# Attention: three sums of sixteen moved from VectorE to TensorE, a ring of twelve places, the product with v eight units behind

## The chip, the cores and the metric

The kernel runs on one core of one Trainium2 chip. The metric is device time in microseconds (us) of the whole kernel. The engines that matter here are TensorE (PE in the profile; PEld is its loading of weights), VectorE (DVE), ScalarE (ACT), GpSimd (POOL) and SyncE (SP), which issues most DMAs. Each engine takes its instructions strictly in the order in which they are written and waits for the others by semaphores.

## The reference, cut to what matters

The reference is four residual layers on x of shape (8, 256, 16, 16). The change lies in the second, an attention with 32 heads of 8 channels and 256 positions. The softmax runs over the batch (`axis=0`), not over the keys:

```python
qkv = jnp.einsum('brnd,ed->brne', xr, w_qkv) + b_qkv
q, k, v = jnp.split(qkv, 3, axis=-1)
attn = jnp.einsum('brnd,brmd->brnm', q, k)
attn = jax.nn.softmax(attn, axis=0)
out = jnp.einsum('brnm,brmd->brnd', attn, v)
```

So for each head and each pair of positions eight numbers are exponentiated and divided by their sum: maximum and sum go over the eight batches, element by element.

## The kernel before, in words

**Units.** A unit is one head and one 128 x 128 block of its positions (keys on the partitions, queries along the row), for all eight batches: 128 x 1024 numbers. A head has four units, four heads make a group of 16 units (`UPG`), and eight groups (`NG`) make 128 units (`UNITS`). U is the unit's number, u its place in its group.

**What is done to a unit.** TensorE computes the scores with eight bf16 matmuls into two of the eight PSUM banks (`scores`, L1684; three units have room, `SLOT`). VectorE takes the maximum over the batches (`maximum`, L1042). TensorE subtracts it with two matmuls by a negated identity (`subtract`, L1693). ScalarE takes the exponential into a place of the ring `e_ring` in SBUF (`exponentials`, L644). VectorE sums over the batches (`total`, L1049). ScalarE takes the logarithm of the sum and the exponential of its negative, which is the reciprocal (`logarithm` L649, `inverse` L655). GpSimd multiplies the unit by it in place (`weights`, L459). TensorE multiplies it with v into bank 6, eight fp32 matmuls, four of them side by side on 32 columns each (`product`, L1712).

**Order.** `attention_steps` runs every engine through turns. In turn U TensorE issues the scores of U, the subtraction of U-1 and the product of U-5 (`LAG`); VectorE the maximum of U and the sum of U-1; ScalarE the exponential of U-1, then logarithm and inverse of U-2; GpSimd the weights in the order of U. Nothing is reordered. The ring has eight places (`ER`): the exponential of U waits until the product of U-8 has read its place. The reciprocals have four places (`RS`).

**Once in a group.** After the product of a group's last unit ScalarE copies bank 6 to SBUF (`evacuate`, L664), TensorE transposes it in four matmuls into bank 7 (`transpose_heads`, L1723), and VectorE adds that to x (`add_heads`, L1068, seven times; the eighth group follows the last unit in halves). In the kernel before that is in turns 4, 6 and 7 of the next group.

**Beginning and end.** The q and k parts lie first in the ring and in `scratch`, and SyncE stores them to DRAM, from `scratch` in two DMAs of 1536 KB; a wait of SyncE (L388) stands for both before it loads the second group's heads (L361). At the end VectorE multiplies half of unit 126 and all of unit 127 itself (`normalise_last`, L1054).

## Time and profile before

| what | us |
|---|---|
| median of 3 runs (lowest, highest) | 599.51 (599.00, 599.76) |
| profiled execution, its own time | 600.21 |
| its span in the profile | 598.2 |
| busy in the span: TensorE, VectorE | 504.8 (84%), 481.1 (80%) |
| busy in the span: ScalarE, GpSimd | 328.3 (55%), 387.7 (65%) |
| attention, first maximum to last product | 91.3 to 392.1 |

The span is what the profiler recorded of one execution; 2.0 us of that execution's own time lie outside it. The shares are means over layers with different limits: in the attention stretch VectorE and GpSimd are busy nearly all the time, after it TensorE is. Starts of the matmuls are recorded and their ends are modelled, so a step of TensorE is best read from one start to the next.

### The profile page before, as it was taken

The page shows a single profiled execution, that of the slowest core. Times are in us where ns is not written, and L with a number is a line of the kernel's source. Part 1 is how long each engine was busy: PE and PEld are TensorE (multiplying, and loading weights), DVE is VectorE, ACT ScalarE, POOL GpSimd, SP SyncE. Part 2 cuts the span into 40 slices and gives each one's busy share as a digit, 9 for nine tenths or more (in the row PEclk, how much of TensorE's full clock was granted, in tenths as well). Part 3 has the DMA queues.
Part 4 walks back from the last instruction along what each step waited for, and adds up shares of the span by engine and source line. Part 5 has one row for each costly group of instructions (what it writes and reads, how often), then busy time and mean ns, then how long its engine had stood idle before and what let it go on. Part 6 is the DMA issues. An engine that isn't in the chain of part 4 may idle for free.

```text
span 598.2 us, 13058 instructions
## 1 busy us (share of the span) xinstructions
PE 504.8 (84%) x4610; PEld 308.1 (52%) x4611; DVE 481.1 (80%) x876; ACT 328.3 (55%) x709; POOL 387.7 (65%) x243
## 2 busy tenths in 40 slices
PE   3999687877877778777777877799999999999996
PEld 1554354444444444444444444468986656656665
DVE  5658967999999999999999999978777873333455
ACT  3624674676676766767667676624433533333341
POOL 3200483999899998999999899923105267766640
PEclk9998895999899999999999899999999999999999
DMA  7130257244243332332433320000013223322276
GB/s 225 37 110 1 85 167 253 81 124 130 78 112 84 94 105 73 112 98 80 106 88 93 96 78 2 2 1 1 2 55 101 71 75 107 99 87 90 83 290 211
DMA packets 34288, 56.62 MB, mean 95 GB/s; under 512 B 8541, under 2 KB 21494, under 8 KB 34102
## 3 DMA queue, kind: packets, MB, share of 16 engines
q1 hardware_dynamic: 28950, 43.95, 24.8%
q0 software_dynamic: 3744, 10.39, 5.6%
q10 hardware_dynamic: 1536, 1.51, 0.8%
q8 instruction: 37, 0.61, 0.4%
q14 instruction: 21, 0.17, 0.1%
HBM read 38.43 MB, written 17.40 MB: 93 GB/s over the span
## 4 chain that ended last, share of the span: by engine, by line
PE 37%; POOL 29%; DVE 17%; issue 10%; ACT 3%; DMA 3%; POOLq 0%; SPq 0%; ACTq 0%; DVEq 0%
POOL e_ring L459 29%; PE ps L1890 12%; PE ps L1911 6%; DVE m_bf L1042 4%; DVE x_hat L1049 4%; PE ps L1693 2%; PE ps L1820 2%; DVE stats L865 2%; PE ps L1879 2%; ACT e_ring L644 1%; PE ps L1900 1%; PE ps L1590 1%; PE ps L1621 1%; PE ps L1839 1%; PE ps L1767 1%
## 5 line engine op out<-in xcount | busy, mean ns | idle before, releaser
L459 POOL TENSOR_TENSOR e_ring<-e_ring,x_hat 128x1024 f32<-128x1024 f32 (+1 forms) x127 | 269.8, 2127 | 30.7 <-ACT x_hat L655 18.5
L644 ACT ACTIVATE e_ring<-ps 128x1024 f32<-128x1024 f32 x128 | 131.1, 1025 | 89.7 <-PE ps L1693 89.5
L1042 DVE TENSOR_REDUCE m_bf<-ps 128x128 bf16<-128x1024 f32 x128 | 154.9, 1211 | 4.2 <-PE ps L1684 4.2
L1049 DVE TENSOR_REDUCE x_hat<-e_ring 128x128 f32<-128x1024 f32 x128 | 154.5, 1207 | 3.2 <-ACT e_ring L644 3.2
L1693 PE MATMUL ps<-m_bf,ident_neg 128*128 128x512 bf16 x256 | 82.2, 404 | 61.7 <-DVE m_bf L1042 61.5
L1712 PE MATMUL ps<-e_ring,v_slot 128*32 128x128 f32 x2048 | 86.5, 286 | 1.1 <-POOL e_ring L459 0.6
L1684 PE MATMUL ps<-q_stack,k_stack 72*128 72x128 bf16 x1024 | 83.4, 227 | 3.9 <-DMA k_stack<-qk_parts 3.9
L1712 PEld LDWEIGHTS ps<-e_ring,v_slot 128*32 128x32 f32 x2048 | 50.4, 110 | 58.0 <-issue 51.1
L1684 PEld LDWEIGHTS ps<-q_stack,k_stack 72*128 72x128 bf16 x1024 | 61.9, 101 | 32.0 <-issue 25.8
L1890 PE MATMUL ps<-w_sb,e_ring 128*128 x156 | 74.0, 598 | 1.3 <-ACT e_ring L744 0.8
L477 POOL DMA_INDIRECT e_ring<-token_rows,slot_x x39 | 37.7, 966 | 43.2 <-DVE slot_y L1331 29.5
L1693 PEld LDWEIGHTS ps<-m_bf,ident_neg 128*128 128x128 bf16 x256 | 15.6, 100 | 82.2 <-DVE m_bf L1042 82.0
L1407 DVE TENSOR_TENSOR scratch<-ps,e_ring 128x256 f32<-128x256 f32 x39 | 16.5, 424 | 47.9 <-ACT e_ring L750 47.6
L483 POOL DMA_INDIRECT pair_rows<-scratch,slot_y x37 | 37.8, 1020 | 25.7 <-DVE scratch L1414 14.7
L750 ACT ACTIVATE e_ring<-ps 128x256 f32<-128x256 f32 x39 | 15.0, 384 | 50.0 <-PE ps L1890 49.8
L655 ACT ACTIVATE x_hat<-x_hat 128x128 f32<-128x128 f32 x128 | 39.6, 309 | 4.0
L1911 PE MATMUL ps<-w_sb,scratch 128*128 x156 | 40.5, 382 | 1.2 <-issue 0.6
L649 ACT ACTIVATE x_hat<-x_hat 128x128 f32<-128x128 f32 x128 | 38.5, 301 | 0.7 <-DVE x_hat L1049 0.7
L1890 PEld LDWEIGHTS ps<-w_sb,e_ring 128*128 128x128 f32 x156 | 26.6, 190 | 22.1 <-issue 21.9
L453 POOL TENSOR_TENSOR e_ring<-e_ring 128x512 bf16<-128x512 f32 x8 | 9.1, 1158 | 42.0 <-ACT e_ring L588 41.7
L744 ACT ACTIVATE e_ring<-ps 128x256 f32<-128x256 f32 x39 | 14.9, 383 | 27.8 <-PE ps L1879 27.8
L1911 PEld LDWEIGHTS ps<-w_sb,scratch 128*128 128x128 f32 x156 | 26.7, 190 | 4.7 <-issue 2.7
(237 smaller groups left out, 674.2 us busy)
## 6 DMA issues: line engine op xcount, KB each, us to landing
q_stack<-qk_parts SPq DMA_DIRECT2D x32, 288.0 KB
k_stack<-qk_parts SPq DMA_DIRECT2D x32, 288.0 KB
w_sb<-in_w13T_dram SPq DMA_DIRECT2D x16, 256.0 KB, 7.6
qk_parts<-e_ring SPq DMA_DIRECT2D x8, 384.0 KB, 3.4
qk_parts<-scratch SPq DMA_DIRECT2D x2, 1536.0 KB, 19.7
x_res<-in_x_dram SPq DMA_DIRECT2D x8, 256.0 KB, 3.9
w_sb<-in_w2T_dram SPq DMA_DIRECT2D x8, 256.0 KB, 7.5
work<-pair_rows SPq DMA_DIRECT2D x8, 256.0 KB, 4.7
```

Of the source, the lines that this page charges most:

```text
L459: nc.gpsimd.tensor_tensor(ev, ev, view(x_hat, CH + (u % RS) * P, [[0, quads], [1, P], [0, 2]]), ALU.mult).then_inc(norm_done, 1)
L483: nc.gpsimd.indirect_dma_start(out=y_dram[:, :], in_=y_rows[:, k % YR], in_offset=None, out_offset=bass.IndirectOffsetOnAxis(ap=slot_y[:, ...
L644: nc.scalar.activation(e_ring[:, u % ER, :].rearrange("p (q n k) -> p q n k", q=BQ, k=2), view(ps, 2 * (v % SLOT) * CH, [[2 * P, BQ], [1, ...
L649: nc.scalar.activation(s_ln[:, u % 2], s_sum[:, u % 2], ACT.Ln).then_inc(ln_done, 1)
L655: nc.scalar.activation(s_inv[:, u % RS], s_ln[:, u % 2], ACT.Exp, scale=-1.0).then_inc(r_done, 1)
L1042: nc.vector.tensor_reduce(m_bf[:, u % 2], view(ps, 2 * (v % SLOT) * CH, [[1, P], [P, B]]), AX, ALU.max).then_inc(max_done, 1)
L1049: nc.vector.tensor_reduce(s_sum[:, u % 2], by_position(e_ring[:, u % ER, :]), AXY, ALU.add).then_inc(sum_done, 1)
L1684: last = nc.tensor.matmul(view(ps, 2 * (v % SLOT) * CH + b * P, [[1, P]]), k_stack[:, i, b * N + mh * P:b * N + (mh + 1) * P], q_stack[:, ...
L1693: last = nc.tensor.matmul(bank(2 * (v % SLOT) + j), ident_neg[:], view(m_bf, (u % 2) * P, [[0, B // 2], [1, P]]), start=False, stop=True, ...
L1712: last = nc.tensor.matmul(ps[32 * (b % 4):32 * (b % 4) + 32, 6, (b // 4) * N + nh * P:(b // 4) * N + (nh + 1) * P], v_slot[:, b * H + mh, ...
L1890: last = nc.tensor.matmul(bank(r % 2), x_turned[:, r % 2, h * P:(h + 1) * P], w13_sb[:, h, bass.ds(e * (2 * C), 2 * C)], start=(h == 0), s ...
L1911: last = nc.tensor.matmul(ps[:, 6 + r % 2, 0:C], gated_t[:, r % 2, f * P:(f + 1) * P], w2_sb[:, f, bass.ds(e * C, C)], start=(f == 0), sto ...
```

## The change: what it does

Three things are changed together. **Sums on TensorE:** for the units with u = 0, 5 and 10 (in the first group 5 and 10, in the last only 0; 21 units in all) the sum over the batches is no longer VectorE's. TensorE adds the eight batch blocks into bank 7 with eight fp32 matmuls by the identity (`partial_sum`), four in turn U+2 and four in turn U+3, each four behind the subtraction and ahead of the product of that turn; ScalarE takes the logarithm straight from PSUM at the beginning of turn U+4. Bank 7 is also where the heads are transposed, so the sum of u = 10 waits for `add_heads`, and the transposes for the logarithm of u = 5. **Lags:** VectorE's other 107 sums come two turns behind their unit (one turn for units 0 to 4), logarithm and inverse a turn later, and the product eight turns behind. Evacuation, transposes and `add_heads` move to turns 7, 10 and 11. **Room:** the ring gets twelve places, the last four in `scratch`; the exponential of unit 8, the first that is put there, waits for the two stores out of `scratch`. The reciprocals get eight places. At the end VectorE multiplies unit 125 as well; GpSimd's loop is written out.

```diff
-    ER = 8
-    LAG = 5
-    RS = 4
+    RING, MORE = 8, 4
+    ER = RING + MORE
+    LAG = 8
+    RS = 8
+    TURN_AT = 10
...
+        def attention_steps(step):
+            for U in range(UNITS + LAG):
+                step(U, lambda k: 0 <= U - k < UNITS)
+        def summed_on_pe(U):
+            return U % UPG in ((5, 10) if U < UPG else (0,) if U // UPG == NG - 1 else (0, 5, 10))
+        DVE_SUMS = [U for U in range(UNITS) if not summed_on_pe(U)]
+        PE_SUMS = [U for U in range(UNITS) if summed_on_pe(U)]
+        SUM_BANK, SUM_STEPS, SUM_AT = 7, 2, 2
+        DVE_LAST = {UNITS - 3: 0, UNITS - 2: BQ // 2, UNITS - 1: 0}
+        def sum_step(U):
+            return U + (1 if U < PE_SUMS[0] else 2)
+        def slot_of(U):
+            k = U % ER
+            return (e_ring, k * UW) if k < RING else (scratch, (k - RING + 1) * UW)
...
+                nc.gpsimd.tensor_tensor(ev, ev, view(x_hat, CH + (p % RS) * P, [[0, quads], [1, P], [0, 2]]), ALU.mult
                                         ).then_inc(norm_done, 1)
-            with pool.Fori(0, NG - 1) as g:
-                for u in range(UPG):
-                    weights(g * UPG + u, u)
-            for u in range(UPG - 2):
-                weights((NG - 1) * UPG + u, u)
-            weights(UNITS - 2, UPG - 2, BQ // 2)
+            for p in range(UNITS):
+                if p not in DVE_LAST:
+                    weights(p)
+                elif DVE_LAST[p]:
+                    weights(p, DVE_LAST[p])
...
+                if U >= ER:
                     act.wait_ge(pv_done, U - ER + 1)
-                elif U == 2:
+                elif U in (2, RING):
+                    h = 0 if U == 2 else 1
                     for s in range(2):
-                        act.wait_ge(parts_out[s], 16 * NCH)
-                nc.scalar.activation(e_ring[:, u % ER, :].rearrange("p (q n k) -> p q n k", q=BQ, k=2),
-                                     view(ps, 2 * (v % SLOT) * CH, [[2 * P, BQ], [1, P], [P, 2]]), ACT.Exp).then_inc(exp_done, 1)
-            def logarithm(U, u):
-                act.wait_ge(sum_done, U + 1)
-                nc.scalar.activation(s_ln[:, u % 2], s_sum[:, u % 2], ACT.Ln).then_inc(ln_done, 1)
-            def inverse(U, u):
+                        act.wait_ge(parts_out[2 * h + s], 16 if h else 16 * NCH)
...
+            def logarithm(U):
+                if summed_on_pe(U):
+                    act.wait_ge(pe_sum_done, PE_SUMS.index(U) + 1)
+                    total = ps[:, SUM_BANK, 0:P]
+                else:
+                    act.wait_ge(sum_done, DVE_SUMS.index(U) + 1)
+                    total = s_sum[:, DVE_SUMS.index(U) % 2]
+                nc.scalar.activation(s_ln[:, U % 2], total, ACT.Ln).then_inc(ln_done, 1)
...
+            def attention_step(U, has):
+                g, u = U // UPG, U % UPG
+                late = U - SUM_AT - SUM_STEPS
+                if 0 <= late < UNITS and summed_on_pe(late):
+                    logarithm(late)
+                    inverse(late)
                 if has(1):
-                    exponentials(U - 1, v - 1, (u - 1) % UPG)
-                if has(2):
-                    logarithm(U - 2, (u - 2) % UPG)
-                    inverse(U - 2, (u - 2) % UPG)
-                if u == LAG - 1 and has(LAG):
+                    exponentials(U - 1)
+                for done in (U - 2, U - 3):
+                    if 0 <= done < UNITS and not summed_on_pe(done) and sum_step(done) + 1 == U:
+                        logarithm(done)
+                        inverse(done)
+                if u == LAG - 1 and g >= 1:
                     evacuate(g)
-                if u in (0, 1, 2, LAG) and has(u + 1) and has(0):
...
+                n = DVE_SUMS.index(U)
+                if n >= 2:
+                    dve.wait_ge(ln_done, DVE_SUMS[n - 2] + 1)
+                nc.vector.tensor_reduce(s_sum[:, n % 2], ring(U, [[2, P], [2 * P, BQ], [1, 2]]), AXY, ALU.add).then_inc(sum_done, 1)
...
+                    maximum(U)
+                for done in (U - 1, U - 2):
+                    if 0 <= done < UNITS and not summed_on_pe(done) and sum_step(done) == U:
+                        total(done)
+                if u == TURN_AT + 1 and 1 <= g < NG:
                     add_heads(g, g)
-            attention_steps(dve, attention_step)
-            normalise_last(UNITS - 2, BQ // 2)
-            normalise_last(UNITS - 1, 0)
+            attention_steps(attention_step)
+            for U, first in DVE_LAST.items():
+                normalise_last(U, first)
...
+            def partial_sum(U, step):
+                n = PE_SUMS.index(U)
+                if step == 0:
+                    pe.wait_ge(exp_done, U + 1)
+                    if n >= 1:
+                        pe.wait_ge(ln_done, PE_SUMS[n - 1] + 1)
+                    if U % UPG == 10 and U >= UPG:
+                        pe.wait_ge(x2_added, U // UPG)
+                for b in range(step * (B // SUM_STEPS), (step + 1) * (B // SUM_STEPS)):
+                    last = nc.tensor.matmul(ps[:, SUM_BANK, 0:P], ident[:],
+                                            ring(U, [[2, P]], (b // 2) * (2 * P) + b % 2),
+                                            start=(b == 0), stop=(b == B - 1))
+                if step == SUM_STEPS - 1:
+                    last.then_inc(pe_sum_done, 1)
+            def product(U):
...
+                if summed_on_pe(group * UPG + 5):
+                    pe.wait_ge(ln_done, (group * UPG + 5) + 1)
...
                 if has(0):
-                    scores(U, v, u, g)
+                    scores(U)
                 if has(1):
-                    subtract(U - 1, v - 1, (u - 1) % UPG)
+                    subtract(U - 1)
+                for step in range(SUM_STEPS):
+                    summed = U - SUM_AT - step
+                    if 0 <= summed < UNITS and summed_on_pe(summed):
+                        partial_sum(summed, step)
                 if has(LAG):
-                    product(U - LAG, (u - LAG) % UPG, g)
-                if isinstance(U, int) and U == UNITS + 2:
+                    product(U - LAG)
+                if U == UNITS + LAG - 3:
                     keep_busy(IDLE_BANK, 1)
-                if u == LAG + 1 and has(LAG + 2):
+                if u == TURN_AT and 1 <= g < NG:
                     transpose_heads(g)
```

The instructions of TensorE around the addition of the heads in the second group, first of the kernel before (L1684 scores, L1693 subtraction, L1712 product; turn 24):

```order
L1684 MATMUL ps<-q_stack,k_stack 128x128 [waits exp_done,stack_in2]
L1684 MATMUL ps<-q_stack,k_stack 128x128 x7
L1693 MATMUL ps<-m_bf,ident_neg 128x512 [waits max_done]
L1693 MATMUL ps<-m_bf,ident_neg 128x512
L1712 MATMUL ps<-e_ring,v_slot 32x128 [waits norm_done]
L1712 MATMUL ps<-e_ring,v_slot 32x128 x7
```

and of the change (L1714 scores, L1723 subtraction, L1738 the new sum by the identity, L1758 product; from the subtraction of turn 28 on):

```order
L1723 MATMUL ps<-m_bf,ident_neg 128x512 [waits max_done]
L1723 MATMUL ps<-m_bf,ident_neg 128x512
L1738 MATMUL ps<-e_ring,ident 128x128 [waits x2_added,ln_done,exp_done]
L1738 MATMUL ps<-e_ring,ident 128x128 x3
L1758 MATMUL ps<-scratch,v_slot 32x128 [waits norm_done,v_slot_ready1]
L1758 MATMUL ps<-scratch,v_slot 32x128 x7
L1714 MATMUL ps<-q_stack,k_stack 128x128 [waits exp_done]
L1714 MATMUL ps<-q_stack,k_stack 128x128 x7
L1723 MATMUL ps<-m_bf,ident_neg 128x512 [waits max_done]
L1723 MATMUL ps<-m_bf,ident_neg 128x512
L1738 MATMUL ps<-e_ring,ident 128x128 x4
L1758 MATMUL ps<-scratch,v_slot 32x128 [waits norm_done]
```

Four matmuls of the sum now stand between the subtraction and the product, and the next scores stand behind them; the first four of this unit wait for `x2_added`, the end of `add_heads`.

VectorE at the same place, before (L1042 maximum, L1049 sum, L1068 `add_heads`; turns 23 and 24):

```order
L1042 TENSOR_REDUCE m_bf<-ps 128x128 [waits sub_done,scores_done]
L1049 TENSOR_REDUCE x_hat<-e_ring 128x128 [waits ln_done,exp_done]
L1068 TENSOR_TENSOR x_res<-x_res,ps 128x16x32 [waits acc_tr]
L1042 TENSOR_REDUCE m_bf<-ps 128x128 [waits sub_done,scores_done]
L1049 TENSOR_REDUCE x_hat<-e_ring 128x128 [waits ln_done,exp_done]
```

and in the change (L1068 is now the maximum, L1076 the sum, L1095 `add_heads`; turns 27 to 29):

```order
L1068 TENSOR_REDUCE m_bf<-ps 128x128 [waits sub_done,scores_done]
L1076 TENSOR_REDUCE x_hat<-e_ring 128x128 [waits ln_done,exp_done]
L1095 TENSOR_TENSOR x_res<-x_res,ps 128x16x32 [waits acc_tr]
L1068 TENSOR_REDUCE m_bf<-ps 128x128 [waits sub_done,scores_done] x2
L1076 TENSOR_REDUCE x_hat<-e_ring 128x128 [waits ln_done,exp_done]
```

Where a sum has gone to TensorE two maxima follow each other, here right behind `add_heads`.

## Rows read from the trace of the kernel before

**Rows 1.** Windows, one group: length; busy of PE, PEld, DVE, ACT, POOL; clock; DMA
```profile
244.80:281.50 36.70, 28.50 (x422) 15.63 (x423) 36.70 (x34) 25.78 (x54) 34.15 (x17) 1.00 0.36 95
```
**Rows 2.** Timeline of VectorE at an `add_heads`: start, duration, line, operation
```profile
258.11 0.67 DVE L1068 TENSOR_TENSOR x_res<-x_res,ps 128x512 f32<-128x512 f32 x1
258.71 1.21 DVE L1042 TENSOR_REDUCE m_bf<-ps 128x128 bf16<-128x1024 f32 x1
259.84 1.21 DVE L1049 TENSOR_REDUCE x_hat<-e_ring 128x128 f32<-128x1024 f32 x1
```
**Rows 3.** Timeline of TensorE, one turn behind that `add_heads`; idle time in brackets
```profile
259.98 0.61 PE L1693 MATMUL ps<-m_bf,ident_neg 128*128 128x512 bf16 x2 [1.10 <-DVE m_bf L1042]
260.51 0.66 PE L1712 MATMUL ps<-e_ring,v_slot 128*32 128x128 f32 x16
261.11 0.62 PE L1684 MATMUL ps<-q_stack,k_stack 72*128 72x128 bf16 x8
262.23 0.61 PE L1693 MATMUL ps<-m_bf,ident_neg 128*128 128x512 bf16 x2 [0.50 <-DVE m_bf L1042]
```
**Rows 4.** Timeline of TensorE at the lower clock, and the turn after it
```profile
151.25 1.04 PE L1693 MATMUL ps<-m_bf,ident_neg 128*128 128x512 bf16 x2 [0.50 <-DVE m_bf L1042]
152.22 1.08 PE L1712 MATMUL ps<-e_ring,v_slot 128*32 128x128 f32 x16
153.24 1.03 PE L1684 MATMUL ps<-q_stack,k_stack 72*128 72x128 bf16 x8
154.06 0.85 PE L1693 MATMUL ps<-m_bf,ident_neg 128*128 128x512 bf16 x2
...
155.45 0.62 PE L1684 MATMUL ps<-q_stack,k_stack 72*128 72x128 bf16 x8
155.91 0.60 PE L1693 MATMUL ps<-m_bf,ident_neg 128*128 128x512 bf16 x2
```
**Rows 5.** Windows of TensorE: length, busy, granted clock, DMA
```profile
152.00:154.00 2.00, 2.00 (x25) 0.50 0.13 51
223.00:224.00 1.00, 1.00 (x6) 0.50 0.45 117
336.00:337.00 1.00, 1.00 (x10) 0.50 0.20 70
```
**Rows 6.** The line of `add_heads`: ns min/median/max, first and last start
```profile
L1068 DVE TENSOR_TENSOR x_res<-x_res,ps x7: 671/674/676, 147.1 to 368.6; 128x512 f32<-128x512 f32 x7
```
**Rows 7.** Timeline of TensorE, fp32 matmuls of 128 columns (two records each)
```profile
76.73 0.61 PE L1630 MATMUL ps<-qkv_sb,x_hat 128*128 128x128 f32 x4
77.17 1.02 PE L1621 MATMUL ps<-x_hat,qkv_sb 128*128 128x512 f32 x2
...
84.09 0.68 PE L1630 MATMUL ps<-qkv_sb,x_hat 128*128 128x128 f32 x4 [0.24 <-DVE work L979]
84.61 1.02 PE L1621 MATMUL ps<-x_hat,k_wT_sb 128*128 128x512 f32 x2
```
**Rows 8.** The line of the maximum: ns min/median/max, first and last start
```profile
L1042 DVE TENSOR_REDUCE m_bf<-ps x128: 1205/1211/1225, 91.3 to 385.0; 128x128 bf16<-128x1024 f32 x128
```
**Rows 9.** SyncE's waits: total, times, longest; then its next issue
```profile
SPq L388 <- DMA qk_parts<-scratch: 20.7, 1, 20.7
...
116.80 0.72 SPq L361 DMA_DIRECT2D q_stack<-qk_parts  x1
```
**Rows 10.** Timeline of ScalarE: the exponential of unit 8
```profile
112.93 1.02 ACT L644 ACTIVATE e_ring<-ps 128x1024 f32<-128x1024 f32 x1 [0.69 <-PE ps L1693]
```
**Rows 11.** Timeline, the last weights on VectorE and the last product
```profile
389.10 2.29 DVE L1054 TENSOR_TENSOR e_ring<-e_ring,x_hat 128x512 f32<-128x512 f32 x2
...
391.44 0.66 PE L1712 MATMUL ps<-e_ring,v_slot 128*32 128x128 f32 x16 [0.47 <-DVE e_ring L1054]
```
**Rows 12.** Chain that ended last: GpSimd's weights without a wait between
```profile
158.68 2.01 POOL e_ring L459
160.78 2.15 POOL e_ring L459
```

More of the change, by code:

```diff
@@ L292, in slot_steps, with ring @@
                 step(s, s % XR, inside)
-        def attention_steps(eng, step):
-            for u in range(UPG):
-                step(u, u, u, 0, lambda k: k <= u)
-            for U in range(UPG, UNITS):
-                step(U, U, U % UPG, U // UPG, lambda k: True)
-            for u in range(LAG):
-                step(UNITS + u, UNITS + u, u, NG, lambda k: k > u)
+        def attention_steps(step):
[12 more added lines that the diff above has]
+            return (e_ring, k * UW) if k < RING else (scratch, (k - RING + 1) * UW)
+        def ring(U, dims, first=0):
+            buf, at = slot_of(U)
+            return view(buf, at + first, dims)
         def score_banks(v):
@@ L313, in row_bank @@
             return 5 if j < B // 2 else 4 + j % 2
-        def later_than(U, k):
-            return not isinstance(U, int) or U >= k
-        assert (SLOTS - 7) % XR == 0 and UPG % ER == 0
+        assert (SLOTS - 7) % XR == 0 and CH <= UW and (MORE + 1) * UW <= 6144
         block = ctx.enter_context(nc.Block())
@@ L1069, in add_heads, with attention_step @@
                                         ALU.add).then_inc(x2_added, 1)
-            def attention_step(U, v, u, g, has):
+            def attention_step(U, has):
+                g, u = U // UPG, U % UPG
                 if has(0):
-                    maximum(U, v, u)
-                if has(1):
-                    total(U - 1, (u - 1) % UPG)
-                if u == LAG + 2 and has(LAG + 3):
+                    maximum(U)
[3 more added lines that the diff above has]
+                if u == TURN_AT + 1 and 1 <= g < NG:
                     add_heads(g, g)
-            attention_steps(dve, attention_step)
-            normalise_last(UNITS - 2, BQ // 2)
-            normalise_last(UNITS - 1, 0)
+            attention_steps(attention_step)
+            for U, first in DVE_LAST.items():
+                normalise_last(U, first)
             dve.wait_ge(x2_added, NG - 1)
@@ L1675, in _, with scores @@
                 qk_tile(n)
-            def scores(U, v, u, g):
+            def scores(U):
+                g, u = U // UPG, U % UPG
                 i, mh, nh = u // 4, (u // 2) % 2, u % 2
@@ L1688, in scores, with subtract @@
                 last.then_inc(scores_done, 1)
-            def subtract(U, v, u):
+            def subtract(U):
                 pe.wait_ge(max_done, U + 1)
                 for j in range(2):
-                    last = nc.tensor.matmul(bank(2 * (v % SLOT) + j), ident_neg[:],
-                                            view(m_bf, (u % 2) * P, [[0, B // 2], [1, P]]), start=False, stop=True,
+                    last = nc.tensor.matmul(bank(2 * (U % SLOT) + j), ident_neg[:],
+                                            view(m_bf, (U % 2) * P, [[0, B // 2], [1, P]]), start=False, stop=True,
@@ new lines, in product @@
+            def product(U):
+                grp, u = U // UPG, U % UPG
+                i, mh, nh = u // 4, (u // 2) % 2, u % 2
+                if U % 4 == 0:
+                    pe.wait_ge(v_slot_ready[i], grp + 1)
+                if U % UPG == 0 and U >= 1:
+                    pe.wait_ge(acc_out, grp)
+                if U in DVE_LAST:
+                    pe.wait_ge(norm_last, list(DVE_LAST).index(U) + 1)
+                    if DVE_LAST[U]:
+                        pe.wait_ge(norm_done, UNITS - len(DVE_LAST) + 1)
@@ L1713, in product @@
                                             v_slot[:, b * H + mh, i, :],
-                                            view(e_ring, (u % ER) * UW + (b // 2) * (2 * P) + b % 2, [[2, P]]),
-                                            start=(u == 0 and b < 4), stop=(u == UPG - 1), skip_group_check=True)
+                                            ring(U, [[2, P]], (b // 2) * (2 * P) + b % 2),
+                                            start=(U % UPG == 0 and b < 4), stop=(U % UPG == UPG - 1), skip_group_check=True)
                 last.then_inc(pv_done, 1)
```

60 lines of the change are left out of this document (24 added, 36 removed).

## Prediction

> **What bounds the kernel now.** I read the windows first: in a group of 16 turns VectorE is busy in all of the 36.70 us, GpSimd in 34.15, TensorE in 28.50, ScalarE in 25.78 [rows 1]. The timeline of VectorE then shows no gap: instructions follow each other by 1.13, behind `add_heads` by 0.60 [rows 2]; 32 x 1.128 + 0.60 = 36.7, the whole group. So VectorE sets the pace, a turn is 2.26, and the other engines wait for it: TensorE idles 0.50 before each subtraction, 1.10 behind `add_heads` [rows 3]. GpSimd takes a turn when it need not wait in 2.10 [rows 12], 33.6 a group.
>
> **What the sums cost where they leave.** 21 sums of 1.128 go, 23.7 us. VectorE keeps 128 maxima and 107 sums, 235 x 1.128 = 265.1, and seven `add_heads` of 0.60 [rows 2, 6], 4.2: 269.3 in all. That is the gain if nothing else waits. A group with three fewer is 33.3, about GpSimd's 33.6, so all three engines come close together and what counts is who waits for whom.
>
> **What a sum costs on TensorE.** Eight fp32 matmuls of 128 columns, four to a turn; I call four a piece. The trace has two such matmuls between neighbours in 0.44 [rows 7], so 0.88 for a piece, and in 0.52 behind a wait, so 1.04. What the hand-over from a subtraction adds no row shows; I take 0.93, which is nearest to the undisturbed row, and keep 0.88 and 1.04 as the ends.
>
> **What waits for a piece.** From rows 3 and 4: maximum's start to subtraction 1.27, subtraction to product 0.53, product to scores 0.60, scores to subtraction 0.46 when nothing is awaited (155.45 to 155.91), scores' start to the next maximum 0.65 (0.62 and a signal). A turn of TensorE is thus 1.59, with a piece 2.52, against VectorE's 2.26, or 1.13 in the turn without a sum. Queued behind the piece are the product and the next scores, and VectorE's next maximum waits for these.
>
> Let s be a unit summed on TensorE and 0 the subtraction of s+1, in turn s+2. The maximum of s+1 began at -1.27, that of s+2 at 0.99; without a sum between, VectorE is ready for that of s+3 at 2.12. TensorE: piece 0.53 to 1.46, product to 2.06, scores of s+3, ready at 2.71. VectorE waits 0.59. Next turn: subtraction 2.52, piece 3.05 to 3.98, product to 4.58, scores ready at 5.23; VectorE (2.71 + 2.26) is ready at 4.97 and waits 0.26. In the turn after that scores are ready at 6.82, VectorE at 7.49: over. So a sum saves 1.13 and costs 0.85.
>
> For u = 10 in groups 1 to 6 the first piece also waits for `add_heads`, which stands between the sum of u = 9 and the maximum of u = 12: it begins at 0.99, ends 0.67 later, and the piece starts at 1.70 instead of 0.53. Product, scores and subtraction stand behind it. The maximum of 13 can start at 3.88 while VectorE is ready at 2.72: 1.16, and 0.26 in the next turn. 1.42 for 1.13 saved.
>
> Of the 21 units, 6 are of this second kind, 15 of the first; I count unit 5 with the start. 14 x 0.85 + 6 x 1.42 = 20.4.
>
> **Start.** The exponential of unit 8 now waits for the stores out of `scratch`; SyncE's wait for these ends at 116.80, while the exponential ran at 112.93 before [rows 9, 10]. With 1.02 it ends at 117.9. Behind it on ScalarE are logarithm and inverse of unit 6 and later exponentials; three units of scores fit into PSUM, so TensorE stops before scores 11. VectorE can by then have done maxima 0 to 10 and seven sums, 18 x 1.128 = 20.3, since 91.3 [rows 8]: 26.6 passed, 6.3 idle. GpSimd gets unit 6 only at about 118.5; 119 weights at 2.10 from there end at 368, earlier than VectorE needs them.
>
> **End.** VectorE's last sum ends at 91.3 + 269.3 + 6.3 + 20.4 = 387.3; before it began the weights at 389.10 [rows 11]. It now does one more whole unit, 1.2 (an estimate: the pair took 2.29, half of it possibly waiting), so the last product starts at 387.3 + 1.2 + 2.29 + 0.05 = 390.8 against 391.44 [rows 11], 0.6 earlier. The transposes in turn 10, the copy in turn 7 and the twelve places cost and bring nothing: the idle 0.50 [rows 3] covers four transposes of 0.11 (an estimate by one record of rows 7), and GpSimd never kept TensorE waiting in a steady turn. If that cover goes, about 0.4 a group is added.
>
> The Trainium skill bears on the unit added at the end: by SBUF — State Buffer, section "SBUF: two separate sides", a VectorE operation with two SBUF inputs and a GpSimd operation exclude each other for a whole instruction. The trace fits in that half a unit and a whole one took 2.29 [rows 11], about as much as two whole ones. By that rule the sum would be later by up to one instruction of GpSimd, 2.1 [rows 12].
>
> **The clock.** At the lower clock a turn takes 0.97 + 1.02 + 0.82 = 2.81 instead of 1.59 [rows 4]. Its falls were short (granted clock 0.50 [rows 5]) and came shortly after three of the seven `add_heads`: these run from 147.1 to 368.6 [rows 6], so some 36.9 apart, the third near 220.9 and the sixth near 331.7. Behind each of the seven TensorE idles as in rows 3. Before, TensorE's spare hid nearly all of it. Now the idling before the piece of u = 10 is as long (subtraction's end 0.60 to 1.70) and the fall would meet pieces. If it begins with the first piece, that takes 1.86, product 1.02, scores are ready at 5.64; the second piece at full clock 0.93, the maximum of 14 at 8.11 instead of 6.40: 1.7. If it begins with the subtraction of 12 it is 1.6. Six places x 3/7 x 1.65 = 4.2.
>
> The Trainium skill (TensorE: Matmul & The Clock Gate, section "Why this matters for your kernels") warns only of longer idle gaps; by it no fall is due here and the time would be that of the second rival below. The trace disagrees, three times.
>
> **Sum.** The profiled execution took 600.21, the median is 0.7 lower. 600.2 - 0.6 + 4.2 = 603.8; against the median 603.1.
>
> **Rivals.** *Pieces are hidden.* If the scores come in time after all, the 20.4 go: 599.5 - 0.6 - 20.4 = 578.5, where GpSimd's 33.6 a group is nearly the bound too. For it: TensorE would be busy only 28.5 + 6 x 0.93 = 34.1 of 36.7. Against it: the order of TensorE's queue. Chance 0.13; half hidden, about 589, 0.17.
> *The clock stays up* because the pieces fill TensorE: 599.5 - 0.6 = 598.9, with pieces of 0.88 2.0 less (20 sums x 2 x 0.05). 0.17. This is also the change without effect.
> *Every one of the six gaps brings a fall*, with pieces of 1.04: 598.9 + 6 x 1.65 + 20 x 2 x 0.11 = 613. The longer idle stretch and the start, where TensorE waits some 2 us for the exponential of 8, speak for it; 0.08. It decides as soon as four gaps bring falls, 605.5.
> My forecast, some falls: 0.45, own range 600 to 608.
>
> **Numbers.** About 0.2% (1.2 us) is what can be told from no change. Faster: 0.30 and a little of the third case, 0.33. Same: 0.14. Slower: 0.53. The range reaches from 586, which leaves out most of the first rival, to 610.
>
> **What would show it.** Right: VectorE idle before the maxima of s+3 (0.6, and 1.2 behind `add_heads`) with scores as releaser, a group at about 36 us, the piece at 0.93, the exponential of unit 8 at 116.8, falls of the granted clock at turn 12 with a group of some 38. Wrong: a group under 35 us with VectorE or GpSimd gapless, or the clock at 1.00 throughout.

## Result and profile after

The changed kernel took 607.06 us (median of 4 runs, 606.53 to 609.06) against 599.25 for the one before beside it (4 runs, 598.88 to 599.76): a ratio of 1.0136, 95% interval 1.0111 to 1.0161. It is slower by 7.8 us; forecast were 3.6. The profiled execution of after took 606.7 for a span of 604.9; that of before 600.21 for 598.2. In the profiles, which the rest compares, the difference of the spans is 6.7. One execution of g1 below took 854.93 at a granted clock of 0.56, where its others had 0.96 or more; it is left out of every number.

Four points of the trace split the span: VectorE's first maximum, its last, and the first addition of the last heads behind the last product (L1061 before, L1088 after).

| stretch | before | after | change | forecast |
|---|---|---|---|---|
| start of the program to the first maximum | 91.35 | 89.92 | -1.43 | 0 |
| first to last maximum | 293.64 | 297.07 | +3.43 | +2.0 |
| last maximum to the addition of the last heads | 8.09 | 11.91 | +3.82 | +1.6 |
| from there to the end | 205.12 | 206.00 | +0.88 | 0 |
| span | 598.2 | 604.9 | +6.70 | +3.6 |

The forecast column is worked out from the prediction's own sums: VectorE ready at 387.3 + 4.2, less four instructions of 1.128, puts the last maximum at 386.99; last product at 390.8 + 4.2, and 1.64 from there to the addition, as before.

Windows of after, one group with the granted clock at full speed and one with a fall (columns as in [rows 1], which they answer):

```profile
203.28:239.93 36.65, 32.59 (x476) 21.92 (x468) 33.90 (x31) 25.70 (x54) 33.80 (x17) 1.00 0.34 95
239.93:278.09 38.16, 34.09 (x476) 22.96 (x468) 33.90 (x31) 25.68 (x54) 33.78 (x17) 0.96 0.34 91
```

VectorE has three instructions fewer and 2.8 us less work, but the group is as long as before: 2.75 us of it are now gaps. No engine is busy throughout, so the bound is a chain between two. The waits (total, times, longest) name it:

```profile
PE ps L1723 <- DVE m_bf L1068: 27.7, 53, 1.8
DVE m_bf L1068 <- PE ps L1714: 25.6, 25, 2.9
```

TensorE waits for the maximum, and the maximum for TensorE's scores; before, only the first of the two was of weight (the second came to 4.2). VectorE behind `add_heads` (L1095), answering to [rows 2]:

```profile
229.76 0.68 DVE L1095 TENSOR_TENSOR x_res<-x_res,ps 128x512 f32<-128x512 f32 x1
230.35 1.22 DVE L1068 TENSOR_REDUCE m_bf<-ps 128x128 bf16<-128x1024 f32 x1
232.92 1.22 DVE L1068 TENSOR_REDUCE m_bf<-ps 128x128 bf16<-128x1024 f32 x1 [1.34 <-PE ps L1714]
234.06 1.21 DVE L1076 TENSOR_REDUCE x_hat<-scratch 128x128 f32<-128x1024 f32 x1
235.40 1.23 DVE L1068 TENSOR_REDUCE m_bf<-ps 128x128 bf16<-128x1024 f32 x1
```

and TensorE beside it, answering to [rows 3]; L1738 is a piece (four fp32 matmuls, two records each):

```profile
228.78 0.61 PE L1723 MATMUL ps<-m_bf,ident_neg 128*128 128x512 bf16 x2 [0.50 <-DVE m_bf L1068]
230.59 1.15 PE L1738 MATMUL ps<-scratch,ident 128*128 128x128 f32 x8 [1.21 <-DVE x_res L1095]
231.66 0.66 PE L1758 MATMUL ps<-e_ring,v_slot 128*32 128x128 f32 x16
232.26 0.62 PE L1714 MATMUL ps<-q_stack,k_stack 72*128 72x128 bf16 x8
232.72 0.60 PE L1723 MATMUL ps<-m_bf,ident_neg 128*128 128x512 bf16 x2
233.15 1.07 PE L1738 MATMUL ps<-scratch,ident 128*128 128x128 f32 x8
234.15 0.66 PE L1758 MATMUL ps<-e_ring,v_slot 128*32 128x128 f32 x16
```

The maxima of 230.35 and 232.92 have no sum between them, so VectorE would be back after 1.13; it comes back after 2.57 and waits 1.34 by the row, which counts the maximum as 1.22. The reason is the order of one queue: the scores at 232.26 need nothing of the piece or of the product ahead of them, but stand behind both, and the piece stood 1.21 until `add_heads` had read the bank.

In three of the six groups with this place the granted clock fell there, to 0.50 (the level of 1.2 GHz), while pieces ran. TensorE in one of them, answering to [rows 4], and windows of the other two, answering to [rows 5] (length, busy of five engines, clock, DMA):

```profile
192.44 1.82 PE L1738 MATMUL ps<-e_ring,ident 128*128 128x128 f32 x8 [1.20 <-ACT e_ring L661]
194.20 1.08 PE L1758 MATMUL ps<-e_ring,v_slot 128*32 128x128 f32 x16
195.21 1.03 PE L1714 MATMUL ps<-q_stack,k_stack 72*128 72x128 bf16 x8
```
```profile
268.00:272.00 4.00, 4.00 (x37) 3.04 (x37) 1.42 (x3) 0.49 (x1) 2.13 (x2) 0.60 0.36 102
305.00:309.00 4.00, 3.61 (x32) 2.99 (x33) 1.38 (x2) 0.76 (x3) 3.28 (x2) 0.57 0.58 166
305.39:308.20 2.81, 2.81 (x24) 2.34 (x24) 0.99 (x1) 0.37 (x2) 2.81 (x2) 0.50 0.64 176
```

The first row names ScalarE as the releaser; but the exponential that ended at 192.30 is the next unit's, which the piece does not need, and `add_heads` ended at 192.30 too. In all six groups the piece began 0.14 or 0.15 behind the end of `add_heads`.

Piece 1.76, product 1.01, scores 1.03: the interval between the two maxima was 4.07 in this fall, against 2.56 or 2.57 in the three groups without one. From maximum to maximum the eight groups took 37.72, 37.11, 36.71, 37.17, 36.71, 36.71, 37.06, 34.45 before (the last has 15 intervals) and 38.58, 36.64, 38.14, 36.65, 38.16, 38.12, 36.64, 34.14 after.

The end of attention, answering to [rows 11]: VectorE, GpSimd, TensorE.

```profile
386.99 1.22 DVE L1068 TENSOR_REDUCE m_bf<-ps 128x128 bf16<-128x1024 f32 x1
388.12 3.47 DVE L1076 TENSOR_REDUCE x_hat<-e_ring 128x128 f32<-128x1024 f32 x3
391.50 3.75 DVE L1081 TENSOR_TENSOR e_ring<-e_ring,x_hat 128x1024 f32<-128x1024 f32 x3
...
389.16 3.29 POOL L477 TENSOR_TENSOR e_ring<-e_ring,x_hat 128x1024 f32<-128x1024 f32 x2 [0.61 <-ACT x_hat L677]
...
393.58 0.69 PE L1758 MATMUL ps<-e_ring,v_slot 128*32 128x128 f32 x16 [1.44 <-DVE e_ring L1081]
394.20 2.08 PE L1666 MATMUL ps<-ones_sb 128*128 128x512 f32 x2
396.20 1.70 PE L1758 MATMUL ps<-e_ring,v_slot 128*32 128x128 f32 x32
```

VectorE is through with the weights at 395.25. The products of units 126 and 127 do not follow: a filler matmul (L1666, there to keep TensorE busy) is in the queue ahead of them, and takes 2.08 at the lower clock instead of 1.13. The same filler in the kernel before, and the clock from VectorE's last weights to the addition of the heads in the changed one (0.69; before, 1.00):

```profile
389.08 1.13 PE L1637 MATMUL ps<-ones_sb 128*128 128x512 f32 x2
```
```profile
395.26:398.90 3.64, 3.64 (x40) 2.00 (x39) 1.53 (x7) 0.66 (x2) 0.00 (x0) 0.69 0.00 0
```

### The profile page after: what moved, and what is told of

Same layout as the page of the kernel before. It is cut to its first block, busy times and chain, and to the rows that moved or that the text cites. A ratio compares the mean times of both kernels' runs of the same rounds, so it can differ in the third digit from the quotient of the medians.

```text
span 604.9 us, 13580 instructions
## 1 busy us (share of the span) xinstructions
PE 537.5 (89%) x4946; PEld 357.2 (59%) x4947; DVE 463.0 (77%) x856; ACT 327.7 (54%) x709; POOL 383.2 (63%) x242
## 4 chain that ended last, share of the span: by engine, by line
PE 61%; DVE 22%; DMA 8%; issue 5%; ACT 2%; SPq 1%; POOL 0%; DVEq 0%; ACTq 0%
PE ps L1943 11%; DVE m_bf L1068 9%; PE ps L1758 7%; PE ps L1723 7%; PE ps L1738 7%; PE ps L1714 6%; PE ps L1964 6%; DVE x_hat L1076 4%; DMA qk_parts<-scratch 3%; PE ps L1619 2%; PE ps L1873 2%; PE ps L1932 2%; PE ps L1953 1%; DMA k_stack<-qk_parts 1%; PE ps L1892 1%
## 5 line engine op out<-in xcount | busy, mean ns | idle before, releaser
L477 POOL TENSOR_TENSOR e_ring<-e_ring,x_hat 128x1024 f32<-128x1024 f32 x86 | 181.0, 2128 | 32.6 <-ACT x_hat L677 32.3
L1068 DVE TENSOR_REDUCE m_bf<-ps 128x128 bf16<-128x1024 f32 x128 | 155.9, 1219 | 28.2 <-PE ps L1714 25.6
L661 ACT ACTIVATE e_ring<-ps 128x1024 f32<-128x1024 f32 x88 | 90.1, 1024 | 64.7 <-PE ps L1723 64.3
L1723 PE MATMUL ps<-m_bf,ident_neg 128*128 128x512 bf16 x256 | 80.3, 396 | 27.8 <-DVE m_bf L1068 27.7
L1076 DVE TENSOR_REDUCE x_hat<-e_ring 128x128 f32<-128x1024 f32 x74 | 89.4, 1210 | 1.3 <-ACT e_ring L661 1.3
L477 POOL TENSOR_TENSOR scratch<-scratch,x_hat 128x1024 f32<-128x1024 f32 x40 | 84.7, 2141 | 5.4 <-ACT x_hat L677 5.3
L1714 PE MATMUL ps<-q_stack,k_stack 72*128 72x128 bf16 x1024 | 82.7, 226 | 4.0 <-DMA k_stack<-qk_parts 3.1
L1714 PEld LDWEIGHTS ps<-q_stack,k_stack 72*128 72x128 bf16 x1024 | 61.5, 101 | 31.9 <-issue 25.1
L1758 PE MATMUL ps<-e_ring,v_slot 128*32 128x128 f32 x1408 | 59.0, 287 | 2.1 <-DVE e_ring L1081 1.4
L661 ACT ACTIVATE scratch<-ps 128x1024 f32<-128x1024 f32 x40 | 40.9, 1023 | 28.2 <-PE ps L1723 25.2
L1758 PEld LDWEIGHTS ps<-e_ring,v_slot 128*32 128x32 f32 x1408 | 35.1, 110 | 30.8 <-issue 16.2
L677 ACT ACTIVATE x_hat<-x_hat 128x128 f32<-128x128 f32 x128 | 39.8, 311 | 4.1
L1723 PEld LDWEIGHTS ps<-m_bf,ident_neg 128*128 128x128 bf16 x256 | 17.9, 100 | 38.2 <-DVE m_bf L1068 37.6
L1076 DVE TENSOR_REDUCE x_hat<-scratch 128x128 f32<-128x1024 f32 x33 | 40.0, 1211 | 0.2 <-ACT x_hat L671 0.2
L1738 PEld LDWEIGHTS ps<-e_ring,ident 128*128 128x128 f32 x224 | 32.4, 206 | 10.8 <-ACT e_ring L661 6.7
```

The lines of the kernel that those rows point to most:

```text
L477: nc.gpsimd.tensor_tensor(ev, ev, view(x_hat, CH + (p % RS) * P, [[0, quads], [1, P], [0, 2]]), ALU.mult).then_inc(norm_done, 1)
L661: nc.scalar.activation(ring(U, [[2 * P, BQ], [2, P], [1, 2]]), view(ps, 2 * (U % SLOT) * CH, [[2 * P, BQ], [1, P], [P, 2]]), ACT.Exp).then ...
L677: nc.scalar.activation(s_inv[:, U % RS], s_ln[:, U % 2], ACT.Exp, scale=-1.0).then_inc(r_done, 1)
L1068: nc.vector.tensor_reduce(m_bf[:, U % 2], view(ps, 2 * (U % SLOT) * CH, [[1, P], [P, B]]), AX, ALU.max).then_inc(max_done, 1)
L1076: nc.vector.tensor_reduce(s_sum[:, n % 2], ring(U, [[2, P], [2 * P, BQ], [1, 2]]), AXY, ALU.add).then_inc(sum_done, 1)
L1714: last = nc.tensor.matmul(view(ps, 2 * (U % SLOT) * CH + b * P, [[1, P]]), k_stack[:, i, b * N + mh * P:b * N + (mh + 1) * P], q_stack[:, ...
```

## Experiments

Each is the changed kernel with the edit shown; times are medians, ratios against the kernel before on the same chip (medians 598.7 to 599.3). "End" is the stretch from the last maximum to the addition of the last heads.

**e1. No sums on TensorE.** Lags, ring and end stay.

```diff
-            return U % UPG in ((5, 10) if U < UPG else (0,) ...
+            return False
-            return U + (1 if U < PE_SUMS[0] else 2)
+            return U + (1 if U < 5 else 2)
```

> Keeps the lags, the twelve places, the wait of unit 8 and the end of the change, but gives all 128 sums back to VectorE. Theory (the pieces stand ahead of the next scores in TensorE's queue, and the piece behind add_heads meets falls of the clock): VectorE is gapless again, a group takes 36.7 us, no fall costs more than 0.5; what stays against the kernel before is start and end, so 599 to 604 us. Rival (the lags, the places in scratch and the later product cost the time, not the sums): still 605 or more.

604.97, ratio 1.0099 (1.0070 to 1.0128). The groups 1 to 6 are what the theory said:

```profile
203.80:240.52 36.72, 29.51 (x424) 16.19 (x420) 36.72 (x35) 25.63 (x54) 33.31 (x17) 0.95 0.32 90
```

VectorE gapless at 36.7, and a clock of 0.95 in this group that costs nothing, since TensorE has spare. But the time is all but the rival's 605. The first group took 39.68 (37.72 before), and from the last maximum to the addition of the heads 11.83 (8.09 before): 5.7 us in the two, without a single sum on TensorE. My theory had the sums right and these two places wrong. In the first group it is the exponential of unit 8, the stretch of [rows 9, 10]:

```profile
116.24 1.02 ACT L661 ACTIVATE scratch<-ps 128x1024 f32<-128x1024 f32 x1 [4.78 <-DMA qk_parts<-scratch]
```

**e2. Third sum away from `add_heads`.** u = 13 instead of 10.

```diff
-            return U % UPG in ((5, 10) if U < UPG else (0,) if U // UPG == NG - 1 else (0, 5, 10))
+            return U % UPG in ((5, 13) if U < UPG else (0,) if U // UPG == NG - 1 else (0, 5, 13))
```

> The change with the third sum of each group at u = 13 instead of 10, so that its first piece in turn 15 no longer waits for add_heads in turn 11; the number of matmuls is the same. Theory: each third sum costs VectorE 0.8 us of waiting instead of 1.65 (6 x 0.85 = 5), and the 1.2 us of idling before the piece and with it the three falls of 1.5 us go: 596 to 600 us, the group at 35.8. Rival (TensorE is simply too full, with 24 more fp32 matmuls a group): no change, 605 to 608.

597.66, ratio 0.9963 (0.9940 to 0.9986), as expected. Groups 2 to 6 took 35.87 to 35.89, with the clock at 1.00:

```profile
201.64:237.51 35.87, 32.36 (x469) 22.00 (x468) 33.88 (x30) 25.55 (x53) 33.86 (x17) 1.00 0.36 98
```

Against the 36.64 without a fall this is 0.77, the second kind of wait turned into the first; against 38.1 it is 2.3. From the first to the last maximum 288.97 instead of 297.07: 8.1 us, six of 0.77 and three falls of 1.5 make 9.1, and one fall is left in group 1 (36.72 instead of 35.88).

The end changed too, though nothing there was edited: 10.28 instead of 11.91. The filler still stands ahead of the last two products, but the clock stayed at 1.00:

```profile
386.17 0.67 PE L1758 MATMUL ps<-e_ring,v_slot 128*32 128x128 f32 x16 [2.23 <-DVE e_ring L1081]
386.76 1.13 PE L1666 MATMUL ps<-ones_sb 128*128 128x512 f32 x2
387.82 1.13 PE L1758 MATMUL ps<-e_ring,v_slot 128*32 128x128 f32 x32
```
```profile
387.85:389.92 2.07, 2.07 (x39) 1.51 (x39) 1.53 (x6) 0.66 (x2) 0.00 (x0) 1.00 0.00 0
```

VectorE's last weight ended at 387.85, so the filler was over by then, and from there to the addition it took 2.07, where the changed kernel took 3.64 (1.69 before the change). In f2 and f3 below the clock stayed at 1.00 there as well, and the same stretch took 2.08 in each.

**e3. Scores ahead of the piece.** The scores of the next unit are issued right behind the subtraction.

```diff
-                if has(0):
-                    scores(U)
+                if U == 0:
+                    scores(0)
                 if has(1):
                     subtract(U - 1)
+                if has(-1):
+                    scores(U + 1)
```

> The change with one thing moved: TensorE issues the scores of U+1 right behind the subtraction of U-1, ahead of the pieces and of the product; same instructions, same number. Theory: the next maximum no longer waits for a piece, the 21 us of VectorE's waits go, a group comes down to what GpSimd needs, 33.6 to 34.5 us, and the time to 582 to 590. Rival (TensorE's total work, or contention, is the bound): the waits only move to another place and the time stays above 600.

582.62, ratio 0.9705 (0.9667 to 0.9743). All of the change's sums stay, only the order in TensorE's queue is another, and the gaps on VectorE are gone:

```profile
196.84:230.17 33.33, 31.85 (x470) 22.64 (x469) 33.33 (x32) 25.76 (x53) 33.33 (x17) 1.00 0.39 104
```

33.33 is the 33.3 that the prediction gave for 32 - 3 instructions and an `add_heads`. VectorE and TensorE around a unit summed on TensorE:

```profile
209.25 1.23 DVE L1068 TENSOR_REDUCE m_bf<-ps 128x128 bf16<-128x1024 f32 x1
210.38 1.22 DVE L1076 TENSOR_REDUCE x_hat<-e_ring 128x128 f32<-128x1024 f32 x1
211.51 2.36 DVE L1068 TENSOR_REDUCE m_bf<-ps 128x128 bf16<-128x1024 f32 x2
...
210.54 0.61 PE L1723 MATMUL ps<-m_bf,ident_neg 128*128 128x512 bf16 x2 [0.26 <-DVE m_bf L1068]
210.98 0.61 PE L1714 MATMUL ps<-q_stack,k_stack 72*128 72x128 bf16 x8
211.43 1.12 PE L1738 MATMUL ps<-e_ring,ident 128*128 128x128 f32 x8
```

Two maxima in one stretch of 2.36: the scores at 210.98 are in time, and the piece takes what TensorE had to spare. VectorE and GpSimd are now both busy throughout. This is the forecast's first rival (pieces hidden), which lacked only the order.

**e4. Old end.** The unit added to VectorE's last weights goes back to GpSimd.

```diff
-        DVE_LAST = {UNITS - 3: 0, UNITS - 2: BQ // 2, UNITS - 1: 0}
+        DVE_LAST = {UNITS - 2: BQ // 2, UNITS - 1: 0}
```

> The change with the end of the kernel before: GpSimd multiplies unit 125 again and VectorE only half of 126 and 127. Theory (VectorE's weights of unit 125 wait for GpSimd's running instruction and take 2.0 us, and the filler matmul behind runs at the lower clock): last product 2 to 3 us sooner after the last maximum, 603.5 to 605.5 us. Rival (the end is as long either way, because GpSimd is later with 125 than VectorE): 606 to 608.

608.89, ratio 1.0147 (1.0103 to 1.0192): no gain, the theory on the end falls. The unit was not what made the end longer (11.79 from the last maximum to the addition, against 11.91): VectorE is 0.8 later with its last weight, and TensorE takes 0.9 less behind it. The line of VectorE's last weights (ns min/median/max), after and here:

```profile
L1081 DVE TENSOR_TENSOR e_ring<-e_ring,x_hat x3: 679/1212/2019, 391.5 to 394.0; 128x1024 f32<-128x1024 f32 x2, 128x512 f32<-128x512 f32 x1
```
```profile
L1081 DVE TENSOR_TENSOR e_ring<-e_ring,x_hat x2: 2177/2311/2445, 393.3 to 395.7; 128x512 f32<-128x512 f32 x1, 128x1024 f32<-128x1024 f32 x1
```

Beside GpSimd's weights half a unit and a whole one take over 2.1; with GpSimd done, 0.68 and 1.21. This run had four falls in its six groups.

**f1. Scores ahead, ring of eight, product seven behind.** The edit of e3, and:

```diff
-    RING, MORE = 8, 4
+    RING, MORE = 8, 0
-    LAG = 8
+    LAG = 7
```

> The scores-ahead version (582.6 us) with the ring cut back to eight places and the product with v seven units behind. Exponential 8 then writes a place of the first eight and waits for no store. Theory (the lags and the room cost time at the start only because exponential 8 waits for the scratch stores): the first group, 41.1 us in the scores-ahead run with one interval of 4.49, falls to about 37 to 39, the later groups stay at 33.3, and the time is 578 to 581. Rival (eight places are too few once VectorE turns a unit every 1.1 us without a sum, so that exponentials wait for products): groups of 34 us or more, and a time of 583 or more.

580.41, ratio 0.9701 (0.9661 to 0.9741). The first group went from 38.89 to 36.52, the later ones stayed at 33.34: eight places are enough, and the wait for the stores was avoidable. The end was 1.5 longer (13.59 against 12.07), at a clock of 0.53 from the last weights to the addition; the ratios of e3 and f1 have intervals that overlap, so the gain is read from the first group and not from the medians. (The expectations of f1, f2 and f3 give 41.1 and 41.9 for the first group of e3 and e1: these counted 17 intervals where a group has 16. The right numbers are 38.89 and 39.68.)

**f2. No sums on TensorE, VectorE's sum one behind.** The edit of e1, but:

```diff
-            return U + (1 if U < 5 else 2)
+            return U + 1
```

> The version without any sum on TensorE (604.97 us), with VectorE's sum one unit behind instead of two; the ring of twelve and the product eight behind stay. Theory (the lag of the sum leaves one sum more after the last maximum and, at the start, the wait of exponential 8 stops VectorE either way): last maximum to last product about 1.1 us shorter, first group within 0.5 us of 41.9, time 603 to 604.5. Rival (the lag of two is what starves VectorE at the start, where the order maximum, sum of two before lets exponential and sum fall apart): first group about 38 and a time of 600 to 601.

604.55, ratio 1.0091 (1.0060 to 1.0121). Neither number of mine: the first group took 41.31, 1.6 longer than with the sum two behind, and the end 9.60, 2.2 shorter. One interval is 5.77 where e1's longest is 4.55: the lag of two is no cost at the start; most likely it leaves VectorE a sum more to do while exponential 8 waits. Of the 2.2 at the end, VectorE's weights ended 0.7 sooner behind the last maximum (7.53 against 8.20), and 1.55 is the clock, which stayed at 1.00 there (2.08 from the last weight to the addition against 3.63).

**f3. No sums on TensorE, ring of eight, product seven behind.**

> The version without any sum on TensorE (604.97 us), with the ring cut back to eight places and the product seven units behind; VectorE's sum stays two behind. Theory (the wait of exponential 8 for the scratch stores, with the falls of the clock behind it, is what makes the first group 41.9 instead of 37.7): first group about 37.7, end as in the version it comes from less the one product that is no longer left, time 600 to 601.5. Rival (the start costs the same without that wait, for instance by the lag of the sum): first group above 40 and a time of 603.5 or more.

601.65, ratio 1.0033 (1.0014 to 1.0052). Edits of e1 and f1 together. First group 38.09, end 10.28: 1.6 of the 2.0 at the start were the wait for the stores, nearly what the theory said. The end is 1.55 shorter than in e1, again with the filler in place and the clock at 1.00.

**f4. Scores ahead without the filler** three turns before the end. The edit of e3, and:

```diff
-                if U == UNITS + LAG - 3:
-                    keep_busy(IDLE_BANK, 1)
```

> The scores-ahead version (582.6 us) without the one filler matmul of TensorE that stands three turns before the end. Theory (that filler, 2.08 us at the lower clock, stands between VectorE's last weights and the last two products): the last product comes about 1 to 1.5 us earlier and the time is 581 to 582. Rival (the filler ends before the last weights are ready, or without it the clock is lower in the products): within 0.5 us of 582.6.

580.63, ratio 0.9699 (0.9661 to 0.9737). The end went from 12.07 to 11.33, 0.7 of the 2.0 by which the medians differ. The rest is not shown to be the edit's: the runs of e3 lie between 579.51 and 584.93, and the two intervals overlap.

**g1. The changed kernel without the filler.**

> The changed kernel (607.1 us) without the one filler matmul of TensorE three turns before the end. Theory (the end's miss is this filler: 2.08 us between the product of unit 125 and the last two, which VectorE's weights had released 0.95 us before they ran): last maximum to the end of the last product 9.2 to 9.7 us instead of 10.9, the groups as before (36.64, or 38.1 with a fall of the clock), time 605 to 606. Rival (the filler was cover, and without it the last products run at the lower clock): within 0.5 us of 607.1.

The edit shown at f4, without that of e3. 606.82 (five executions), ratio 1.0126 (1.0102 to 1.0150): in the median 0.24, which is the rival's number; in the trace the end is 10.77 instead of 11.91, 1.14 shorter, as the theory said.

```profile
394.77 2.81 PE L1758 MATMUL ps<-e_ring,v_slot 128*32 128x128 f32 x48 [1.45 <-DVE e_ring L1081]
397.52 1.22 PE L1666 MATMUL ps<-ones_sb 128*128 128x256 f32 x2
```

The last three products now stand together, but at the lower clock in part, as the 1.22 of the next filler shows (0.70 at full speed). The first maximum came at 90.99 instead of 89.92, and that hides the gain in the span (605.0). Over the 14 profiles shown or told here the first maximum lies between 88.9 and 91.6, ahead of anything the edits touch; one us is not to be settled by these medians.

**g2. The changed kernel with the ring of eight and the product seven behind.**

> The changed kernel (607.1 us) with the ring cut back to eight places and the product with v seven units behind, so that exponential 8 waits for no store. Theory (in the version without TensorE's sums this took 1.6 us from the first group and one product from the end): the first group 36.5 to 37.5 instead of 38.6, end 0.3 to 1.5 us shorter, the later groups unchanged in their waits; time 604 to 606. Rival (the twelve places and the eight turns are what the two-step sums need: product 7 behind lets exponentials or weights wait): groups above 36.7 where no clock falls, time 607 or more.

The edit of f1. 607.47, ratio 1.0135 (1.0115 to 1.0156): my theory on the start falls for the changed kernel. The first group took 38.93 instead of 38.58. The wait for the stores is gone, and the piece of unit 5 meets the lower clock, which the start still has until 112:

```profile
106.95 1.92 PE L1738 MATMUL ps<-e_ring,ident 128*128 128x128 f32 x8
108.79 1.08 PE L1758 MATMUL ps<-e_ring,v_slot 128*32 128x128 f32 x16
109.81 1.03 PE L1714 MATMUL ps<-q_stack,k_stack 72*128 72x128 bf16 x8
```

One delay hid the other. The end, forecast to be shorter, took 11.87 against 11.91. The later groups are unchanged (36.63, or 38.0 to 38.15 with a fall), so the rival on the places falls too, though its time came true.

**g3. Scores ahead, ring of eight, no filler.**

> Scores ahead, a ring of eight and no filler together (580.4 with the first two, 580.6 with the first and the last). Theory (the two terms are at different ends of the attention and add up): 578 to 579.5. Rival (the filler's loss hangs on the state of the clock at the end and is gone when the end is reached earlier): 580 to 581.

Edits of e3, f1 and f4. 580.37, ratio 0.9674 (0.9649 to 0.9700). First group 37.24, end 11.21, against 36.52 and 13.59 with the filler; in the median no further gain, the rival's number. Its reason the trace does not bear out: the end is 2.4 shorter, and what hides it are a first group 0.7 longer and a first maximum at 91.56 against 89.24. This or either half of it is the best version, 3% faster than the kernel before.

**g4. The same, with the last group's sums on VectorE and one behind.**

```diff
-            return U % UPG in ((5, 10) if U < UPG else (0,) if U // UPG == NG - 1 else (0, 5, 10))
+            return U < UNITS - UPG and U % UPG in ((5, 10) if U < UPG else (0, 5, 10))
-            return U + (1 if U < PE_SUMS[0] else 2)
+            return U + (1 if U < PE_SUMS[0] or U >= UNITS - UPG else 2)
-                for done in (U - 2, U - 3):
+                for done in (U - 3, U - 2):
-                for done in (U - 1, U - 2):
+                for done in (U - 2, U - 1):
```

> As the version with scores ahead, a ring of eight and no filler, and the last group's sums all on VectorE and one unit behind instead of two (one sum more on VectorE, 1.13 us). Theory (two sums and the maximum are in front of the last weights either way, since VectorE has no gap: what the lag costs at the end is not VectorE's time but the weights of GpSimd that come later): within 1 us of the version with the lag of two. Rival (the lag leaves 1.1 us at the end): 1 us or more faster than it even with the added sum.

581.12, ratio 0.9708 (0.9683 to 0.9732). The end is 0.9 shorter (10.33), the last group 2.6 longer (35.92 instead of 33.33): two sums more stand ahead of the last maximum, the added one and the one that the shorter lag takes out of the end, 2.26, and two short waits. Last group and end together are 1.7 longer. The median is within 1 us of the version above, as the theory said, but the first group was 1.0 shorter in this trace (36.28 against 37.24); the rival, 1 us or more faster, falls.

## Why the prediction was partly wrong

*What bounds; what a sum on TensorE costs.* Right. The piece is 1.00 behind a subtraction (233.15 to 234.15; 0.93 taken, 0.88 and 1.04 the ends); the subtraction hands over in 0.43 instead of 0.53, so the two together came out as 1.43 against 1.46.

*The wait for a piece.* Right for the first kind: the maxima stand 1.71 and 2.49 apart instead of 1.13 and 2.26, a wait of 0.81 against 0.85.

```profile
207.80 1.22 DVE L1068 TENSOR_REDUCE m_bf<-ps 128x128 bf16<-128x1024 f32 x1
209.51 1.23 DVE L1068 TENSOR_REDUCE m_bf<-ps 128x128 bf16<-128x1024 f32 x1 [0.49 <-PE ps L1714]
210.65 1.21 DVE L1076 TENSOR_REDUCE x_hat<-e_ring 128x128 f32<-128x1024 f32 x1
212.00 1.23 DVE L1068 TENSOR_REDUCE m_bf<-ps 128x128 bf16<-128x1024 f32 x1
```

For the second kind 2.57 and 2.48: 1.66 against 1.42, since the piece starts 1.81 behind the subtraction instead of 1.70 and takes 1.07 there. A group without a fall is 36.64; the working gave 36.70 - 3.38 + 1.70 + 1.42 = 36.44. That only the order causes these waits, the scores ahead show.

*The clock.* Right in number and price: three falls in six groups, 1.5 each (38.14 to 36.64), where 3/7 and 1.65 were taken. In the three other runs with u = 10 behind `add_heads` and the scores behind the piece it was 4, 3 and 3 of 6. With u = 13 and with the scores ahead the clock stayed at 1.00 in groups 2 to 6. The rule of the Trainium skill that the prediction weighed (TensorE: Matmul & The Clock Gate, section "Why this matters for your kernels") is again not what the trace shows: TensorE had idled 1.20 or 1.21 just before each of the three.

*Start.* Right: the first group's 38.57 less its 28 instructions of 1.128 leaves 7.0 of waiting, where the working has 6.3 and 0.85 for unit 10. The exponential of unit 8 ran at 115.06, not 116.80, and 1.4 of this is that all of attention began earlier in this execution.

```profile
115.06 1.02 ACT L661 ACTIVATE scratch<-ps 128x1024 f32<-128x1024 f32 x1 [2.87 <-DMA qk_parts<-scratch]
```

The last maximum came at 386.99, the very number of the forecast, and that is luck: the 1.4 pays for six second-kind waits that were 0.24 too small. And g2 shows that the start would have cost the same by the lower clock if the stores had not.

*End.* This is the step that failed. "One more whole unit, 1.2" and 0.05 from VectorE's weights to the last product gave 1.6 more behind the last maximum; it was 3.8, 2.2 more than the step gave. VectorE's part was nearly right (sums until 391.50, weights 3.75 against 3.49), 0.26 of the 2.2. What I left out is on TensorE, which I took to be free and at full clock once VectorE is done: from VectorE's last weight to the addition of the heads it took 3.64, not the 1.69 of before, 1.95 more. Two things make these 1.95, and what each costs depends on the other. The filler is in the queue ahead of the last two products; before, it ran from 389.08 to 390.21, while VectorE was still at its weights, and I did not ask where it stands once these are later. And the clock fell. With the filler but no fall (e2, f2, f3) the stretch is 2.07 or 2.08: the filler's place costs 0.38, the fall the other 1.57. With a fall but no filler (g1) it is 2.54: so counted the filler costs 1.10, the fall 0.85. Why the clock fell at this end in ten of the thirteen profiles of the changed kernel and its variants, and not in e2, f2 and f3, no run here shows.

By e4 the added unit was not to blame: without it GpSimd still works while VectorE wants to, and both take longer. That is the rule of SBUF — State Buffer (section "SBUF: two separate sides") in the Trainium skill, and the trace agrees: the 2.02 of the first weights is 0.95 until GpSimd's end at 392.45 and 1.07 behind it, about what a unit takes alone (1.21).

*The rest.* 0.88 behind the last heads is in no step. In every variant that stretch is 205.7 or more, against 205.12 before; why, no run here shows. The remaining 1.1 of the miss in the medians, 4.2 in all, are the profiled executions: that of before lay 1.0 above its median, that of after 0.4 below, less 0.2 that lies outside the spans.

*Rivals.* "Pieces hidden" needed one edit of the order to come true, at 580.4 to 582.6 where it said 578.5. "The clock stays up" is refuted by three falls, "every gap brings a fall" by three that did not.

## What to carry to other kernels

Work moved to an engine with spare time lands in that engine's queue: ask which instruction behind it somebody waits for, and put that one ahead; here this was worth 24 us, three times what the move itself lost. When the end of a phase moves, walk the queue of every engine there, fillers too: an instruction that was cover before can stand in the way after, here for 0.4 us at full clock and 1.1 at the lower one; and ask at which clock the last work runs, which here weighed 0.85 to 1.57. And check a small gain at one end by the stretch it is in, not by the median, when the phase before varies by more.

## What was not expected of the hardware

- Four fp32 matmuls of 128 columns take 1.00 behind a bf16 subtraction and the hand-over 0.43; behind a wait for another engine 1.07.
- The clock fell behind 1.2 us of TensorE idle in 13 of 24 such places, in the same program at the same place in some groups and not in others; what decides it these runs do not show.
- At the end of attention TensorE idled 1.3 to 2.3 us before the product of unit 125 in all thirteen profiles of the changed kernel and its variants; the clock fell behind it in ten, and stayed at 1.00 in three with idle times of 1.56, 1.56 and 2.23.
- Half a unit of weights on VectorE took 0.68 alone and over 2.1 beside GpSimd's weights.
